# Turned tokens of a gated delta rule: ScalarE writes scaled values and keys straight from PSUM, and the turns stand among output and gate products

## The reference

```
q = silu(conv4(hT @ Wq)); k = silu(conv4(hT @ Wk)); v = silu(conv4(hT @ Wv))   # 96, 96, 192 columns
q = q / sqrt(sum(q*q) + 1e-6) * 96**-0.5;  k = k / sqrt(sum(k*k) + 1e-6)
beta = 2 * sigmoid(hT @ Wb);  g = -exp(A_log) * softplus(hT @ Wa + dt_bias)
per token:  S = S * exp(g);  delta = (v - k @ S) * beta;  S = S + outer(k, delta);  o = q @ S
o = o * rsqrt(mean(o*o) + 1e-6) * norm_weight * silu(hT @ Wg);  x = x + o @ Wo
```

## Time and profile before

| | |
|---|---|
| three runs | 2247.32, 2251.04 and 2253.84 us, median 2251.04 us |
| the profiled execution | 2245.72 us, its span 2243.9 us |
| busy share of the span | PE 95%, VectorE 89%, ScalarE 61%, GpSimd 48% |
| granted TensorE clock, mean | 0.978 of full speed |
| steps 8 to 59 | 1509.93 us, 29.04 us a step |
| GpSimd on V (L834) and K2 (L881) | 146.9 and 160.8 us |

### The profile page before, as it was taken

The page is one execution under the profiler, slowest core; times in us unless marked ns, Lnnn a source line. Parts: engine busy times, 40 slices in busy tenths (PEclk is TensorE's granted clock), DMA queues, the critical chain, the costliest instruction groups (busy, mean ns, idle before and its releaser), DMA issues. The chain is left out here.

```text
span 2243.9 us, 58371 instructions
## 1 busy us (share of the span) xinstructions
PE 2124.5 (95%) x21537; PEld 1488.1 (66%) x21560; DVE 1988.2 (89%) x4323; ACT 1371.3 (61%) x3891; POOL 1083.5 (48%) x1539
## 2 busy tenths in 40 slices
PE   5899999999999999999999999999999998868998
PEld 3576767777767676776767676767676766643544
DVE  8999999999999999999999999999999986467786
ACT  5566666666666666666766767665656554214655
POOL 2545454545445454545454545454545443125554
PEclk8999999999999999999999999999999998788999
DMA  5222333333333333333443333432222222140000
GB/s 141 60 72 74 82 80 76 85 81 85 85 84 81 76 83 89 90 91 90 94 92 92 94 92 96 87 83 61 64 59 52 66 47 60 28 155 18 20 25 29
DMA packets 455176, 169.16 MB, mean 75 GB/s; under 512 B 378310, under 2 KB 433894, under 8 KB 454380
## 3 DMA queue, kind: packets, MB, share of 16 engines
q1 hardware_dynamic: 454892, 165.43, 30.4%
HBM read 83.30 MB, written 56.90 MB: 62 GB/s over the span
## 5 line engine op out<-in xcount | busy, mean ns | idle before, releaser
L1491 DVE SCALAR_TENSOR_TENSOR d_y<-bank,d_cw,d_y 128x508 f32<-128x508 f32 (+2 forms) x576 | 421.4, 732 | 5.5 <-ACT d_y L1253 0.6
L851 POOL TENSOR_SCALAR d_ms<-d_sso 128x4 f32<-128x4 f32 x64 | 14.5, 226 | 538.6 <-ACT d_junk L1392 538.6
L799 POOL TENSOR_TENSOR d_Gm<-cst,gh 128x512 f16<-128x512 f32 x128 | 131.0, 1044 | 183.6 <-DVE d_ohl L1658 180.4
L1260 ACT ACTIVATE d_th<-d_y 128x512 f32<-128x512 f32 x192 | 121.1, 630 | 128.0 <-DVE d_y L1497 104.6
L834 POOL TENSOR_TENSOR d_V<-d_tok,d_kinv 128x640 f32<-128x640 f32 (+1 forms) x128 | 146.9, 1168 | 60.2 <-issue 58.2
L1253 ACT ACTIVATE d_y<-bank,d_cw 128x512 f32<-128x512 f32 x192 | 131.1, 683 | 60.9 <-PE bank L917 58.9
L1664 DVE SCALAR_TENSOR_TENSOR x<-bank,x 128x512 f32<-128x512 f32 x128 | 87.3, 682 | 88.9 <-PE bank L1064 88.9
L881 POOL TENSOR_SCALAR d_K<-d_tok,d_Em 128x96 f32<-128x96 f32 x256 | 160.8, 642 | 0.1
L1302 ACT ACTIVATE d_tok<-bank 128x384 f32<-128x384 f32 x256 | 125.5, 490 | 41.1 <-PE bank L933 37.4
L1382 ACT ACTIVATE d_Dl<-bank 128x384 f32<-128x384 f32 x128 | 62.2, 490 | 116.1 <-PE bank L1040 116.1
L1377 ACT ACTIVATE d_thg<-bank 128x384 f32<-128x384 f32 x128 | 62.0, 484 | 108.1 <-PE bank L1028 107.9
(11 more groups left out here) (337 smaller groups left out, 6612.9 us busy)
## 6 DMA issues: line engine op xcount, KB each, us to landing
normed<-d_ohl SPq DMA_DIRECT2D x64, 384.0 KB, 3.8
lt_blocks<-d_LT SPq DMA_DIRECT2D x64, 256.0 KB, 2.5
d_fw<-turned_gate_w SPq DMA_DIRECT2D x32, 256.0 KB, 3.2
d_XT<-x_blocks SPq DMA_DIRECT2D x128, 64.0 KB, 2.4
d_X<-x_blocks SPq DMA_DIRECT2D x128, 64.0 KB, 2.4
d_fw<-turned_val_w SPq DMA_DIRECT2D x32, 256.0 KB, 3.1
d_fw<-turned_out_w SPq DMA_DIRECT2D x32, 256.0 KB, 2.8
d_st<-in_L_attn_Wg_dram SPq DMA_DIRECT2D x16, 384.0 KB, 4.0
```

Of the source, the lines that this page charges most:

```text
L799: nc.gpsimd.tensor_tensor(Gm[:, w, :, :], over(U, 1, B), over(gh[:, w, n, :], 2, P), ALU.mult).then_inc(s["Gm_ready"], 1)
L1260: nc.scalar.activation(th[:, :, :], y[(st.p + j) % 2][:, :, :], ACT.Tanh).then_inc(s["tanh_done"], 1)
L1491: nc.vector.scalar_tensor_tensor(out=yy[:, :, tap:], in0=pp[:, :, 0:P - tap], scalar=cw[:, ds(st.kp, 1), t, 3 - tap], in1=yy[:, :, tap:], ...
```

## The change

ScalarE's `tokens(st, i)` no longer copies 384 columns to `tok`. It reads bank 2 in four instructions: two that write V for columns 96 to 255 and 352 to 383 scaled by `kinv`, one that writes K2 scaled by the last column of `Em`, and one that squares the queries and sums them (what `norms` did). The tile `tok`, `norms`, GpSimd's `values` and its four K2 instructions go, and K2 becomes a pair of tiles. GpSimd makes `kinv` ahead of `Em`. The first turn of a step stands behind the last level; the other three stand between the two halves of `output`, between output and gates, and behind the gates. Projection parts fill the places between levels that the turns leave. On ScalarE `tokens` stands behind `tanh(1)` and `tap0(2)`. VectorE's `recursion(4)` moves ahead of `low`.

```diff
             def key_decay(m, q):
                 hold(pool, s["Dn_ready"], 5 * m + 5)
+                nc.gpsimd.tensor_scalar(sse[:, :], nsse[:, :], -1.0, None, ALU.mult).then_inc(s["kappa_done"], 1)
+                past(pool, "V_ready", m)
+                hold(pool, s["kappa_done"], 4 * m + 1)
+                nc.gpsimd.tensor_tensor(kinv[:, :], sse[:, :], phalf[:, :], ALU.pow).then_inc(s["kappa_done"], 1)
                 past(pool, "Em_ready", m)
                 past(pool, "PT_ready", m - 1)
+                past(pool, "K2_ready", B * m - B)
                 nc.gpsimd.tensor_tensor(Em[q][:, :, :], over(cst[:, C_NU:C_NU + P], 1, B), over(Dn[:, :], 2, P), ALU.mult).then_inc(s["kappa_done"], 1)
-                nc.gpsimd.tensor_scalar(sse[:, :], nsse[:, :], -1.0, None, ALU.mult).then_inc(s["kappa_done"], 1)
                 past(pool, "E_ready", m + 1)
-                hold(pool, s["kappa_done"], 4 * m + 2)
+                hold(pool, s["kappa_done"], 4 * m + 3)
                 nc.gpsimd.tensor_tensor(Em[q][:, :, :], E[:, :, :], Em[q][:, :, :], ALU.mult).then_inc(s["Em_ready"], 1)
-                past(pool, "V_ready", m)
-                nc.gpsimd.tensor_tensor(kinv[:, :], sse[:, :], phalf[:, :], ALU.pow).then_inc(s["kappa_done"], 1)
-
-            def values(m, q):
-
-                hold(pool, s["kappa_done"], 4 * m + 3)
-                past(pool, "tok_read", B * m + B)
-                past(pool, "d_done", 2 * m - 2)
-                for at, lo, hi in ((V_AT, 0, VM), (VE_AT, VM, DV)):
-                    last = nc.gpsimd.tensor_tensor(V[q][:, :, lo:hi], tok[q][:, :, at:at + hi - lo], over(kinv[:, :], 2, hi - lo), ALU.mult)
-                last.then_inc(s["V_ready"], 1)
...
-                    for i in range(B):
-                        nc.gpsimd.tensor_scalar(K2[:, i, :], tok[st.p][:, i, K_AT:K_AT + DK], Em[st.p][:, i, P - 1:P], None,
-                                                ALU.mult).then_inc(s["K2_ready"], 1)
...
                 elif len(units(n)) == 1:
+                    output(st, 0, 1)
+                    turn(1)
+                    output(st, 1, 2)
+                    turn(2)
+                    gates(st, 0)
+                    turn(3)
...
             def tokens(st, i):
-                m = st.n + 1
+                m, q = st.n + 1, st.pm
                 past(a, "tok_done", B * m + i + 1)
                 if i == 0:
-                    past(a, "V_ready", m - 1)
-                    past(a, "K2_ready", B * st.n)
-                nc.scalar.activation(tok[st.pm][:, i, :], bank[2][:, 0:QKV], ACT.Copy).then_inc(s["tok_read"], 1)
+                    past(a, "kappa_done", 4 * m + 2)
+                    past(a, "d_done", 2 * m - 2)
+                    past(a, "su_done", 2 * m - 2)
+                    past(a, "Em_ready", m + 1)
+                for at, lo, hi in ((V_AT, 0, VM), (VE_AT, VM, DV)):
+                    last = nc.scalar.activation(V[q][:, i, lo:hi], bank[2][:, at:at + hi - lo], ACT.Copy, scale=kinv[:, i:i + 1])
+                if i == B - 1:
+                    last.then_inc(s["V_ready"], 1)
+                nc.scalar.activation(K2[q][:, i, :], bank[2][:, K_AT:K_AT + DK], ACT.Copy, scale=Em[q][:, i, P - 1:P]).then_inc(s["K2_ready"], 1)
+                past(a, "tok_read", B * m - B + i + 1)
+                nc.scalar.activation(sq[:, i, :], bank[2][:, Q_AT:Q_AT + DK], ACT.Square, accum_out=ss[:, i:i + 1]).then_inc(s["tok_read"], 1)
```

More of the change, by code:

```diff
@@ L589, in stage_delta_rule @@
         share = sb("share", [P, 3, B, 3])
-        tok = [sb(f"tok{q}", [P, B, QKV]) for q in range(2)]
         sq = sb("sq", [P, B, DK])
@@ L612, in stage_delta_rule @@
         Dl = sb("Dl", [P, B, DV])
-        K2 = sb("K2", [P, B, DK])
+        K2 = [sb(f"K2{q}", [P, B, DK]) for q in range(2)]
         thg = sb("thg", [P, 2 * DV])
@@ L872, in step @@
                         nc.gpsimd.tensor_copy(bqb[:, :, :], over(bq[:, :], 2, P)).then_inc(s["const_ready"], 1)
[L873 to L889 removed]
+                if st.turn and st.recur:
+                    key_decay(m, st.pm)
+                if st.recur and st.project:
+                    past(pool, "low_ready", n)
+                    exponents(n + 2)
+                if st.turn:
+                    past(pool, "tok_read", B * m + B)
                     nc.gpsimd.tensor_scalar(epsq[st.pm][:, :], ss[:, :], EPS, EPS * DK * NORM, ALU.add, ALU.mult).then_inc(s["kappa_done"], 1)
@@ L1041, in pair_of, with output @@
                 last.then_inc(s[done], 1)
-            def output(st):
+            def output(st, lo=0, hi=4):
                 n = st.n
                 for e, u in enumerate(units(n)):
+                    if not lo <= 2 * e + 1 or not 2 * e < hi:
+                        continue
                     past(pe, f"onT_in{u % 2}", 16 * (u // 2 + 1))
@@ L1050, in output @@
                     for i in range(2):
+                        if not lo <= 2 * e + i < hi:
+                            continue
                         at = (6, 5, 7, 4)[2 * e + i]
@@ L1172, in step @@
                     proj(1, 3, 6)
+                    proj(1, 4, 6)
                     y_32(st)
+                    proj(1, 5, 6)
+                    proj(2, 0, 6)
+                    x_32(st)
+                    proj(2, 1, 6)
+                    proj(2, 2, 6)
+                    proj(2, 3, 6)
+                else:
+                    proj(1, 2, 6)
+                    y_32(st)
+                    proj(1, 3, 6)
                     proj(1, 4, 6)
-                    turn(1)
                     x_32(st)
@@ L1178, in step @@
                     proj(2, 0, 6)
-                else:
-                    y_32(st)
-                    proj(1, 2, 6)
-                    proj(1, 3, 6)
-                    x_32(st)
-                    proj(1, 4, 6)
-                    turn(1)
-                    proj(1, 5, 6)
+                    proj(2, 1, 6)
                 if n == NS - 1:
@@ L1190, in step @@
                 if c:
-                    proj(2, 0, 6)
+                    proj(2, 2, 6)
                 past(pe, "W_ready", B * n + 2)
                 pair_of(st, "qs_done", 0, 4, lambda i: qry[0:DK, i, :], lambda i: S[:, i, :], product=c > 0)
-                turn(2)
                 if c == 0:
-                    for part in (1, 2, 3):
-                        proj(2, part, 6)
+                    proj(2, 4, 6)
+                    proj(2, 5, 6)
                 x_join(st)
                 if c:
-                    proj(2, 1, 6)
+                    proj(2, 3, 6)
                 past(pe, "PT_ready", n + 1)
                 pair_of(st, "qs_done", 1, 7, lambda i: qry[0:DK, i, :], lambda i: S[:, i, :], product=c > 0)
-                turn(3)
+                turn(0)
                 if n == NS - 1:
                     turn_x(1)
-                for part in range(4 if c == 0 else 2, 6):
-                    proj(2, part, 6)
-                if len(units(n)) < 2:
-                    output(st)
+                if c:
+                    proj(2, 4, 6)
+                    proj(2, 5, 6)
                 if n == 0:
                     pe.wait_ge(s["set_read"], 4)
-                gates(st, 0)
-                if len(units(n)) == 2:
+                if not units(n):
+                    turn(1)
+                    gates(st, 0, (0,))
+                    turn(2)
+                    gates(st, 0, (1,))
+                    turn(3)
+                elif len(units(n)) == 1:
+                    output(st, 0, 1)
+                    turn(1)
+                    output(st, 1, 2)
+                    turn(2)
+                    gates(st, 0)
+                    turn(3)
+                else:
+                    turn(1)
+                    gates(st, 0)
+                    turn(2)
                     output(st)
+                    turn(3)
                 past(pe, "XT_ready", n + 1)
@@ L1233, in step @@
                         past(pe, "x_added", added(n))
-                pair_of(st, "su_done", 0, 4, lambda i: K2[:, i, :], lambda i: Dl[:, i, :], rows=DK, product=c < CH - 1)
+                pair_of(st, "su_done", 0, 4, lambda i: K2[st.p][:, i, :], lambda i: Dl[:, i, :], rows=DK, product=c < CH - 1)
                 if st.turn:
@@ L1241, in step @@
                     last.then_inc(s["fgam_done"], 1)
-                pair_of(st, "su_done", 1, 2, lambda i: K2[:, i, :], lambda i: Dl[:, i, :], rows=DK, product=c < CH - 1)
+                pair_of(st, "su_done", 1, 2, lambda i: K2[st.p][:, i, :], lambda i: Dl[:, i, :], rows=DK, product=c < CH - 1)
             all_steps(step)
```

29 lines of the change are left out of this document (11 added, 18 removed).

## The result

The changed kernel takes 2275.1 us (median of 4 runs, 2273.1 to 2277.7) against 2250.2 us for the kernel before in the same comparison, a ratio of 1.0111 with a 95% interval of 1.0096 to 1.0127. The forecast was 2267 us in a range of 2226 to 2300: 16 us more than before, where the measurement has 25. The profiled execution has a span of 2271.3 us against 2243.9.

The account below looks back on a forecast made before the run. PE (95% busy) and VectorE (89%) were both taken as near their limit. 13 groups made +20 us, irregular waits -4, the ends even: +16, stated as 2267 us against 2251.0, range 2226 to 2300.

Parts of the forecast that it names:

- VectorE: VectorE from keyscale to the end of group 1's correction: 13.7 us expected instead of 14.71, by shorter recursion(4) and correction.
- PE between the levels: PE's waits between levels, put at 0.5 to 1.0 us a step: 0.7 us gained in each step.
- The second turn: Turn 1 waits for ScalarE's 1.2 us read until 17.4 us; steps with c = 0 become 2.3 us longer.
- The group of four: One regular head, steps with c = 0 to 3: 117.1 us in place of 115.5, 1.6 longer.
- a term of 0.3 us for ScalarE's read_d: End of steps with c = 1: PE asks for read_d(0) 8.4 us after turn 1, ScalarE needs 8.9.
- The irregular waits: 8 us of irregular waits in the 52 middle steps, half of which may vanish in PE's idle time: -4 us.
- Steps 0 to 7 and 60 to 63 as even: Steps at both ends of the program: taken as neither longer nor shorter.
- The faster one: VectorE reaches tanh(1) 0.7 us sooner still, so PE's own arrival decides in c = 1 to 3: 2232 us, chance 0.25.
- The cancelling one: Gain and loss cancel, the four steps within 0.4 us a group of the old ones: 2251 us, chance 0.10.
- The tail: ScalarE's tail becomes the bound if a read takes 1.47 us, deciding from about 1.3: 2292 us, chance 0.15.
- The 60 us asked for: Mark in the profile after: PE waits more than 60 us in all for ScalarE's turn reads, mostly at c = 0.

Follow-up runs that it names:

- early read: Changed kernel with ScalarE's read of turned token 0 moved ahead of tanh(1): 2236.4 us; the same move with the old copy at the new places: 2230.0 us.
- GpSimd's products back: Changed kernel plus two GpSimd products of V's old size, written to a spare tile at their old place behind Gm: 2321.1 us, ratio 1.0309.

## Why the prediction was right, and where it was off

**The mechanism and the sum.** The main cost was read rightly: turn 1 waits for a read that stands behind tanh(1) and tap0(2), and moving that read takes the whole loss back. The size came out near by errors of both signs. The 52 steps in the middle lost 10.8 us and not 16; everything outside them, priced at nothing, lost 16.6. The upper part of the range, in which the 2275 us lie, had been given for longer reads, which did not come.

**VectorE: right.** recursion(4) is 0.15 us, the correction of group 1 0.17, and from the start of `keyscale` (1367.91) to the end of the correction (1381.56) step 44 has 13.65 us, forecast 13.7. The Trainium skill, page "SBUF — State Buffer", section "SBUF: two separate sides", had been weighed in the prediction with a price of up to 0.3 us a step for the new order of Em behind kinv. The trace agrees: the correction of group 0 rises in steps with c = 0 from 0.17 to 0.46 us (1374.01), while GpSimd's Em product runs from 1373.18 to 1374.45; in c = 1 it is 0.38, in c = 3 still 0.17. In the kernel with the copy at the new places, where Em stands ahead of kinv as before, it is 0.17 in nearly every one of these steps. So this clash is part of the 13.65 us. That the chain would be 0.3 us shorter without it is not shown: the kernel with the copy at the new places has no such clash in step 44 and still takes 13.82 us.

**PE between the levels: this term failed. It was a gain of 0.7 us a step and is between -0.45 and 0.74.** Without three turns of 0.39 the first output matmul of before stands at 13.14, 16.42, 15.67 and 15.78 us of a step with c = 0 to 3 (means 14.31, 17.59, 16.84, 16.95). After, it stands at 13.59, 15.68, 15.65 and 15.65. Only c = 1, which lost its late start, gained; c = 0 lost 0.45. The mark that hardly a wait of PE would be left at L1007 (L992 after) failed too: the weight loads wait 26.9 us there, against 32.2. In steps with c = 1 to 3 it is 0.42 us in the kernel before and in the kernel after, so ScalarE's reads of the turns had not been what made it. In steps with c = 0 a new wait stands in the levels. Projection parts had to fill the places of the turns, so the first part of group 2 is issued early, and its bank is the one of group 0, which ScalarE frees with the copy behind tanh(0):

```profile
1375.39 0.60 PE L902 MATMUL bank<-hhi,d_wa1h 128*128 128x512 f16 x2 [0.97 <-ACT d_tail L1267]
```

It comes in each of the 16 steps with c = 0. The sum over the program, where the kernel before had 0.8 us:

```profile
PE bank L902 <- ACT d_tail L1267: 17.8, 16, 2.9
```

The kernels with the early read have it as well (17.8 and 16.8 us). No run here moved this part elsewhere, so what it is worth to the whole stays open.

**The second turn: the mechanism right, its price too high.** Forecast and measured in a c = 0 step (means): tanh(1) at 15.0 and 14.92, turn 1 at 17.4 and 17.18, the rest of the step behind it 11.9 and 11.92. From the start of the read to turn 1 it is 1.1 us in step 44, not 1.2: two value reads in 0.57 us, the key read, the square and its sum, overlapping, 1.02 us in all. PE reaches the place at 13.59 + 1.94 = 15.53, not 15.05, as the levels gave nothing. So it stands for 1.65 us, not 2.4. In c = 2 and 3 I had PE wait from 16.8 to 17.4; in truth it arrives at 17.6 by itself. The step came out right there with a wrong reason, which the early read shows, as it changes nothing.

**The group of four.** Forecast 29.3, 29.6, 29.3 and 28.9; measured regular 28.80, 29.36, 29.36 and 28.92 (means 29.10, 29.59, 29.36, 28.92). In c = 1 a term of 0.3 us for ScalarE's read_d had been added (its own count, 8.9 us against 8.4, gives 0.5); it is not there, as from turn 1 to the next keys these steps take the same 11.77 us as those with c = 2. The group is 0.90 us longer instead of 1.6, and over 13 groups that is 11.7 instead of 20. The irregular waits fell by 0.9 us, not by 4. Together it is +10.8 for steps 8 to 59, against +16.

**Steps 0 to 7 and 60 to 63 as even: this step failed.** They cost 12.7 us (+8.5, -1.2, +5.2, +0.2), more than the 52 steps between, and 3.8 us more lie before and behind them. I had said that turn 1 is hidden by half of an output product, and had not asked what stands there in steps that have none (0 to 5) or whose two stand behind turn 2 (60). There turn 1 stands behind turn 0 and at most two projection parts, and in step 3 PE waits 1.78 us at turn 1 and 0.87 at turn 3, in step 60 3.37 us at turn 1. The early read takes back 7.3 and 3.5 us of it.

**The rivals.** The faster one needed VectorE to reach tanh(1) 0.7 us sooner; it came as forecast. The cancelling one set its point at a read near 1.0 us and a full 1.0 us from the levels: the read came near it, the levels gave hardly anything. The tail needed 1.3 us a read. Of the marks named ahead, the wait for ScalarE's reads is the largest at turn 1, as said, and 28 of the 42.5 us lie in steps with c = 0. The 60 us asked for are not reached at the matmuls; they are only if the time of the weight loads is taken in (71 us). Steps close to 29 us each came true.

## What to carry to other kernels

When an operation is moved, look at the queue of the engine that must release it: moving the turn cost PE itself next to nothing, and its read two places too late on ScalarE cost 39 us, 17 of them for tap0(2) and the rest for tanh(1), which waits for a third engine. What fills the freed place has a queue behind it too: the projection part that was drawn forward met a bank that was not free yet. Price the irregular steps of a loop by themselves, first of all those in which the work that is to hide the wait doesn't exist. Before replacing a copy by direct writing, try the new places with the old copy: here, with the early read, it gave all of the gain and was shorter on the engine that others wait for.

## What the runs showed of the hardware that I had not expected

- A wait of about 2 us in the middle of dense matmuls can cost more than itself. Behind the 2.00 us at turn 1 the granted clock fell to 0.57 over 4.01 us, and a 128x512 matmul took 0.63 instead of 0.38 us; behind 1.42 us it stayed at 1.00. It is not certain each time: 3 of the 13 steps kept the full clock behind a wait as long or longer, and in the kernel with GpSimd's products back 7 of 13 kept it behind 2.37 us. What else decides it stays open.
- A small VectorE operation on SBUF can last until the end of the GpSimd one beside it: 12 columns took 1.11 us instead of 0.17 (up to 1.26 in the kernel before), and 32 x 8 numbers 0.78 instead of 0.15, both ending within 0.03 us of a product on GpSimd. Shortening GpSimd's work is one cure; letting it run later in the step cured it as well (VectorE's busy time 1908 and 1912 us).
- What such a clash costs hangs on what is queued behind it: with the read of turn 0 behind tanh(1) the same two products cost 46 us, with the read ahead of it 8 us.
